# New slots for the second block's steps beside the attention heads, and score maxima turned as 16 rows of 128

## The chip, the cores and the metric

The kernel runs on one core of one Trainium2 chip. The metric is the time of one launch on the device in microseconds (us), as a median over runs.

## What is computed

Eight independent samples (B = 8), each 512 rows of 512 numbers, go through two transformer blocks, one after the other. Cut to what matters here:

```python
# block 0 (16 heads of 32; every linear layer quantises its input rows to 8 bits and its weight to -1, 0, 1)
xn = rmsnorm(x, g1) * (1 + scale) + shift
q, k, v = heads(bitlinear(xn, w_qkv, b_qkv))
attn = softmax(q @ k.T * 32 ** -0.5)              # 16 heads, each 512 x 512
x = x + bitlinear(attn @ v, w_proj, b_proj)
x = x + bitlinear(gelu(bitlinear(adaln(x), w_fc1)), w_fc2)
# block 1 (one head of 512, plain weights)
h = film(rmsnorm(x), cond)
x = x + softmax(Q(h) @ K(h).T * 512 ** -0.5) @ V(h) @ proj_w + proj_b
x = x + gelu(film(rmsnorm(x), cond) @ mlp_w1 + mlp_b1) @ mlp_w2 + mlp_b2
```

## The kernel before

The instruction streams of all engines are written out by hand. `both(i, j)` on every engine issues block 0 of sample i together with block 1 of sample j = i - 1. So there are nine rounds: sample 0 alone with the preparation of the weights, seven rounds of both, and block 1 of the last sample alone. A round of both lasts some 248 us.

**Precision.** Numbers go to TensorE (PE) as two bf16 parts, high and low. ScalarE (ACT) writes the high part, and VectorE (DVE) or GpSimd (POOL) the low part, as the difference. A product in block 1 is three matmuls for each of four chunks (`three_terms`, L1430 to L1432), twelve of 128x512.

**The heads' loop.** Its order is that of `slots()`: slots (c, n), with n from 0 to 23 for c = 0 and from 0 to 15 for c = 1 to 4. In a slot the PE issues, in this order: block 1's steps that `PE_AT` names for the slot, a late q or k product of block 0 (`LATE_QK`), the scores by query (`scores_by_query`, L1193), the scores by key (`scores_by_key`, L1243, for c > 0), a head's weighing of the values (`weigh_values`, L1278, 32 matmuls), and the turn of a group's maxima (`turn_maxima`, L1212). A group is four heads, so 16 score tiles. The scores by query only serve to find each row's maximum; `maxima` reads them on DVE, two tiles at once for the first 24 (L1202, banks 0 to 3), one at a time for the rest (L1205, banks 0 and 1). The scores by key have two rows more in the contraction, the negated maximum as high and low part, which lie in partitions STACK and STACK + 1 of `q_stack`. ACT takes their exponential (L1250), and the low part of each of the 64 tiles is formed by DVE or POOL (L1261; the lists `LOW_DVE` and `LOW_POOL`). A head's values are weighed seven slots (six in the first group) after the slot of its first exponential, by `VALUES_AT`.

**The way of the maxima of a group c:** DVE writes them into `neg_max` [128 rows, 4 row tiles, 4 heads]. PE turns them, one matmul of 4 columns for each row tile, into a bank of 4 rows (heads) of 512. ACT copies the high part (`max_high`, L1219), DVE takes the low part (`max_low`, L1226), and SyncE (SP) sends each of the two by a DMA of its own into one partition of `q_stack` (`stack_maxima`, L1232 and L1234). The PE waits for both at slot (c + 1, 0) (`scores_by_key`, n == 0). The slots are in `MAX_AT`, `HIGH_AT` and `LOW_AT`.

**Block 1 in the same loop.** Scores of row tiles 2 and 3 (`s1`, `S_AT`), the turned probabilities (`turn_p1`, L1600, `PT_AT`), the four attention outputs (`proj1`, `PROJ_AT`), squares and norms on ACT (L1442, L1458), the turn into columns with film (`turn_y1`, L1477, `TURN_AT`), and eight quarters of the first two products of the first MLP layer (`M_AT`). Their readers on DVE and ACT have slots of their own (`PT_READ`, `PROJ_READ`), or slots derived from the PE's. Engines are independent queues: a slot of DVE is not at the time of the same slot of PE, but its instructions wait in this order.

SP's queue in the loop: spill and stack of q and k parts of group 2 (L1144, L1146, L1155), `stack_maxima` 0, spill 3, `stack_maxima` 1, stack 3, `stack_maxima` 2 and 3.

```python
EXTRA_DVE = (17, 22, 25, 30, 34, 38)
EXTRA_POOL = (48, 52, 56, 60)
LOW_DVE = [e for e in range(KC * HEADS) if (e >= FIRST_DVE or e in EXTRA_DVE) and e not in EXTRA_POOL]   # FIRST_DVE = 42
```

Of the kernel before, what the change touches and what calls it, by code (L numbers as in the profile page):

```python
# [231 lines left out]
def two_blocks(nc, a, out):  # L232
# [6 lines left out]
    with ExitStack() as ctx:  # L239
# [2105 lines left out]
```

## Time and profile before

| | us |
|---|---|
| median of 3 runs | 2208.48 |
| lowest, highest | 2206.46, 2213.61 |
| the profiled execution | 2211.1 |
| its span | 2209.3 |
| PE busy | 1975.2 (89%) |
| DVE busy | 1537.1 (70%) |
| ACT busy | 1088.2 (49%) |
| POOL busy | 807.1 (37%) |

The span runs from the first to the last instruction; 1.8 us lie around it. A matmul's duration in the rows includes its drain: matmuls of 512 columns start 0.22 us apart and are listed with 0.38 us. So idle time of the PE is read from the gaps in the brackets of its rows and from starts, not from the sum of durations.

### The profile page before, as it was taken

How to read it: one execution, taken by the hardware profiler on the slowest of the kernel's cores; microseconds unless marked ns; L12 is line 12 of the kernel's file. 1: busy time of each engine (PE TensorE's matmuls, PEld its weight loads, DVE VectorE, ACT ScalarE, POOL GpSimd, SP SyncE). 2: the span in 40 equal slices, each digit the busy share in tenths (PEclk: the TensorE clock that was granted, in tenths of full speed). 3: DMA queues.
4: the chain of work that ended last, by engine and by line, in shares of the span. 5: the costliest groups of instructions: out<-in, count | busy, mean ns of one | idle time of the engine just before them, and what ended most of it. 6: DMA issues, size and time to landing. Idle time of an engine off the chain costs nothing.

```text
span 2209.3 us, 34388 instructions
## 1 busy us (share of the span) xinstructions
PE 1975.2 (89%) x12991; PEld 981.8 (44%) x12991; DVE 1537.1 (70%) x2667; ACT 1088.2 (49%) x1962; POOL 807.1 (37%) x705
## 2 busy tenths in 40 slices
PE   4787868899988998899988998899988998899989
PEld 3354334544444444544444444544444444544434
DVE  5666567885788767875788767875788767875422
ACT  4475543753456443753456343753456343753230
POOL 2173433741246213741245213741246213741021
PEclk8899889999999999999999999999999999999999
DMA  8442552023321333023321333023321332013212
GB/s 307 146 164 105 191 195 100 26 87 96 129 73 40 105 115 101 26 88 96 132 68 40 107 113 101 26 87 96 131 71 40 109 111 101 26 62 97 91 38 96
DMA packets 152027, 216.97 MB, mean 98 GB/s; under 512 B 74172, under 2 KB 115424, under 8 KB 139704
## 3 DMA queue, kind: packets, MB, share of 16 engines
q1 hardware_dynamic: 144088, 191.66, 26.3%
q10 hardware_dynamic: 7776, 23.10, 2.8%
q8 instruction: 106, 1.74, 0.3%
q14 instruction: 57, 0.47, 0.1%
HBM read 161.97 MB, written 35.72 MB: 89 GB/s over the span
## 4 chain that ended last, share of the span: by engine, by line
PE 55%; DVE 25%; ACT 9%; issue 6%; POOL 3%; DMA 1%; SPq 0%; ACTq 0%; DVEq 0%; POOLq 0%
PE banks L1430 10%; PE banks L1432 10%; PE banks L1431 10%; PE banks L1388 5%; PE banks L1331 4%; DVE memory L1205 4%; PE banks L1278 4%; DVE memory L1202 3%; PE banks L1243 2%; DVE memory L1016 2%; ACT memory L1250 2%; PE banks L1102 2%; PE banks L1193 2%; PE banks L1313 1%; DVE memory L1031 1%
## 5 line engine op out<-in xcount | busy, mean ns | idle before, releaser
L1430 PE MATMUL banks<-memory 128*128 128x512 bf16 x1536 | 586.1, 382 | 25.9 <-DVE memory L1678 5.9
L1431 PE MATMUL banks<-memory 128*128 128x512 bf16 x1536 | 585.5, 381 | 0.0
L1432 PE MATMUL banks<-memory 128*128 128x512 bf16 x1536 | 585.1, 381 | 0.0
L1261 POOL TENSOR_TENSOR memory<-memory 128x512 bf16<-128x512 f32 x332 | 375.4, 1151 | 371.0 <-ACT memory L1250 370.0
L1250 ACT ACTIVATE memory<-banks 128x512 f32<-128x512 f32 x512 | 290.4, 598 | 131.3 <-PE banks L1243 129.1
L1656 POOL TENSOR_TENSOR memory<-memory 128x512 bf16<-128x512 f32 x128 | 153.8, 1204 | 459.1 <-DVE memory L1651 459.1
L1193 PE MATMUL banks<-memory 96*128 96x512 bf16 x512 | 188.6, 395 | 72.8 <-DVE memory L1205 41.4
L1430 PEld LDWEIGHTS banks<-memory 128*128 128x128 bf16 x1536 | 150.7, 98 | 215.3 <-issue 40.0
L1205 DVE TENSOR_REDUCE memory<-banks 128x1 f32<-128x512 f32 x320 | 207.6, 679 | 42.4 <-PE banks L1193 41.9
L1432 PEld LDWEIGHTS banks<-memory 128*128 128x128 bf16 x1536 | 150.8, 98 | 184.0 <-issue 4.4
L1431 PEld LDWEIGHTS banks<-memory 128*128 128x128 bf16 x1536 | 150.9, 98 | 170.5 <-issue 3.5
L1243 PE MATMUL banks<-memory 98*128 98x512 bf16 x512 | 187.6, 391 | 13.3 <-ACT memory L1250 6.7
L1645 ACT ACTIVATE memory<-banks,memory 128x512 f32<-128x512 f32 x128 | 87.5, 684 | 205.1 <-PE banks L1432 135.2
L1678 DVE TENSOR_TENSOR memory<-banks,memory 128x512 f32<-128x512 f32 x128 | 88.2, 689 | 121.3 <-PE banks L1432 120.8
L1278 PEld LDWEIGHTS banks<-memory 128*128 128x128 bf16 x4096 | 145.7, 100 | 47.0 <-issue 24.2
L1261 DVE TENSOR_TENSOR memory<-memory 128x512 bf16<-128x512 f32 x180 | 141.4, 818 | 35.8 <-ACT memory L1250 35.1
L1278 PE MATMUL banks<-memory 128*128 128x66 bf16 x4096 | 152.0, 197 | 14.8 <-issue 12.4
L1651 DVE CAST memory<-memory 128x512 bf16<-128x512 f32 x128 | 67.8, 542 | 93.1 <-ACT memory L1645 92.1
L1331 PE MATMUL banks<-memory 128*128 128x512 fp8e4 x512 | 118.8, 386 | 13.6 <-issue 10.2
L1202 DVE TENSOR_REDUCE memory<-banks 128x2 f32<-128x1024 f32 x96 | 116.8, 1217 | 17.9 <-PE banks L1193 17.1
L1388 PE MATMUL banks<-memory 128*128 128x512 fp8e4 x512 | 118.0, 384 | 8.4 <-DMA memory<-memory 8.4
L1470 POOL TENSOR_TENSOR memory<-memory 128x512 f32<-128x512 f32 x64 | 80.5, 1272 | 119.2 <-DVE memory L1078 112.1
(173 smaller groups left out, 2775.4 us busy)
## 6 DMA issues: line engine op xcount, KB each, us to landing
memory<-weight_parts SPq DMA_DIRECT2D x80, 1024.0 KB, 4.8
memory<-head_parts SPq DMA_DIRECT2D x192, 128.0 KB, 2.6
head_parts<-memory SPq DMA_DIRECT2D x64, 256.0 KB, 2.2
memory<-in_x SPq DMA_DIRECT2D x32, 256.0 KB, 3.4
memory<-ada_rows SPq DMA_DIRECT2D x16, 512.0 KB, 4.5
memory<-in_L_cond_w_fc ACTq DMA_DIRECT2D x2, 4096.0 KB, 14.9
memory<-in_L_cond_mlp_w SPq DMA_DIRECT2D x8, 1024.0 KB, 9.2
weight_parts<-memory SPq DMA_DIRECT2D x8, 1024.0 KB, 5.8
```

Of the source, the lines that this page charges most:

```text
L1193: mm = pe.matmul(banks[:, b], q_stack[0:STACK, c % STACKS, j, t * P:(t + 1) * P], k_stack[0:STACK, c % STACKS, j], start=True, stop=True)
L1202: dve.tensor_reduce(neg_max[:, c % 2, t - 1:t + 1, j], banks[:, b - 1:b + 1], AX.X, ALU.max, negate=True).then_inc(free[b].sem, 1)
L1205: dve.tensor_reduce(neg_max[:, c % 2, t, j:j + 1], banks[:, b], AX.X, ALU.max, negate=True).then_inc(free[b].sem, 1)
L1243: pe.matmul(banks[:, b], k_stack[0:rows, c % STACKS, j, kt * P:(kt + 1) * P], q_stack[0:rows, c % STACKS, j], start=True, stop=True).then_ ...
L1250: act.activation(expo[:, e % RING], banks[:, b], ACT.Exp, scale=HEAD_SCALE).then_inc(free[b].sem, 1)
L1261: eng.tensor_tensor(prob_lo[:, e % RING], expo[:, e % RING], prob_hi[:, e % RING], ALU.subtract).then_inc(ok.sem, 1)
L1278: mm = pe.matmul(banks[:, b, at:at + VALUE], part[:, (h * TT + kt) % RING, t * P:(t + 1) * P], values[:, kt, h], start=(kt == 0 and part i ...
L1331: mm = pe.matmul(banks[:, b], xq[:, k, t * P:(t + 1) * P], w0_fc1[:, k, n * D:(n + 1) * D], start=(k == 0), stop=(k == KC - 1))
L1388: mm = pe.matmul(banks[:, b], hid_turned[t % 2][:, f], w0_fc2[:, f], start=(f == 0), stop=(f == FC - 1))
L1430: pe.matmul(bank, lh, rh, start=(k == 0), stop=False)
L1431: pe.matmul(bank, lh, rl, start=False, stop=False)
L1432: mm = pe.matmul(bank, ll, rh, start=False, stop=(k == KC - 1))
```

## The change

Three things change. (1) `neg_max` is laid out [128 rows, 4 heads, 4 row tiles]; one matmul of 16 columns turns a group's maxima into 16 rows of 128, so `max_high` and `max_low` work on 16 x 128 instead of 4 x 512, and each of the two DMAs moves 16 rows of 256 bytes instead of 4 of 1024 into the same 4096 bytes of one partition. (2) The slots of block 1's steps and of the late q and k steps move, and readers get lists of their own (`FILM_*`, `PT_HIGH`, `PT_LOW`, `S_MAX`, `S_EXP`). `s1` and `proj1` can now be issued in quarters; the four quarters of each stand in one slot. (3) The low parts of 20 instead of 24 tiles are formed by DVE, of 44 instead of 40 by POOL; `ACT_CUTS`, `DVE_CUTS` and `BOUNDS` shift a few steps of block 1 after the loop.

```diff
-LATE_QK = {(0, 6): ("q", 2), (0, 12): ("k", 2), (1, 3): ("q", 3), (1, 6): ("k", 3)}
-LATE_SCALE = {(0, 5): ("q", 2), (0, 9): ("k", 2), (1, 3): ("q", 3), (1, 7): ("k", 3)}
-LATE_HIGH = {(0, 5): ('q', 2), (0, 9): ('k', 2), (1, 4): ('q', 3), (1, 9): ('k', 3)}
-LATE_LOW = {(0, 6): ('q', 2), (0, 12): ('k', 2), (1, 5): ('q', 3), (1, 8): ('k', 3)}
+LATE_QK = {(0, 4): ('q', 2), (0, 12): ('k', 2), (1, 2): ('q', 3), (1, 8): ('k', 3)}
+LATE_SCALE = {(0, 4): ('q', 2), (0, 9): ('k', 2), (1, 2): ('q', 3), (1, 7): ('k', 3)}
+LATE_HIGH = {(0, 4): ('q', 2), (0, 9): ('k', 2), (1, 4): ('q', 3), (1, 10): ('k', 3)}
+LATE_LOW = {(0, 5): ('q', 2), (0, 12): ('k', 2), (1, 4): ('q', 3), (1, 10): ('k', 3)}
...
-M_AT = ((3, 8), (3, 11), (3, 14), (4, 1), (4, 4), (4, 7), (4, 10), (4, 13))
+M_AT = ((3, 11), (3, 13), (3, 15), (4, 2), (4, 3), (4, 5), (4, 9), (4, 15))
...
-ACT_CUTS = (1, 6, 8, 9)
-DVE_CUTS = (2, 3, 4, 6, 8, 9, 10, 11, 12)
-BOUNDS = (14, 14, 15, 16, 17, 18, 19, 20, 21, 22, 23, 24, 25, 26, 27, 27)
+ACT_CUTS = (1, 6, 7, 10)
+DVE_CUTS = (2, 3, 3, 6, 7, 9, 10, 11, 12)
+BOUNDS = (14, 14, 15, 17, 17, 18, 19, 20, 20, 21, 23, 23, 24, 26, 27, 27)
...
-TURN_AT = ((2, 7), (2, 9), (2, 11), (2, 13))
-NORM_AT = ((1, 14), (1, 15), (2, 0), (2, 1))
-SQUARE_AT = ((1, 4), (1, 6), (1, 8), (1, 10))
-PT_AT, PT_READ = (((0, 3), (0, 10), (0, 15)), ((0, 2), (0, 11), (0, 14)))
-S_AT = ((0, 4), (0, 7))
-PROJ_AT, PROJ_READ = (((0, 16), (0, 21), (1, 0), (1, 5)), ((0, 15), (0, 22), (0, 23), (1, 5)))
+TURN_AT, FILM_FULL, FILM_HIGH, FILM_LOW = (((2, 5), (2, 7), (2, 9), (2, 12)), ((2, 5), (2, 7), (2, 9), (2, 12)), ((2, 6), (2, 8), (2, 10), (2, 13)), ((2, 7), (2, 9), (2, 11), (2, 14)))
+NORM_AT = ((1, 14), (1, 15), (2, 0), (2, 2))
+SQUARE_AT = ((1, 0), (1, 1), (1, 5), (1, 11))
+PT_AT, PT_HIGH, PT_LOW = (((0, 3), (0, 10), (0, 16)), ((0, 2), (0, 11), (0, 15)), ((0, 2), (0, 11), (0, 15)))
+S_AT, S_MAX, S_EXP = (((0, 4), (0, 4), (0, 4), (0, 4), (0, 8), (0, 8), (0, 8), (0, 8)), ((0, 4), (0, 8)), ((0, 4), (0, 8)))
+PROJ_AT, PROJ_READ = (((0, 16), (0, 16), (0, 16), (0, 16), (0, 20), (0, 20), (0, 20), (0, 20), (1, 0), (1, 0), (1, 0), (1, 0), (1, 5), (1, 5), (1, 5), (1, 5)), ((0, 17), (0, 20), (0, 23), (1, 5)))
...
-MAX_AT = {(0, 17): 0, (1, 8): 1, (2, 11): 2, (3, 10): 3}
-HIGH_AT = {(0, 17): 0, (1, 9): 1, (2, 10): 2, (3, 9): 3}
-LOW_AT = {(0, 17): 0, (1, 11): 1, (2, 11): 2, (3, 12): 3}
+MAX_AT = {(0, 18): 0, (1, 9): 1, (2, 9): 2, (3, 9): 3}
+HIGH_AT = {(0, 18): 0, (1, 11): 1, (2, 10): 2, (3, 9): 3}
+LOW_AT = {(0, 18): 0, (1, 13): 1, (2, 11): 2, (3, 10): 3}
...
-EXTRA_DVE = (17, 22, 25, 30, 34, 38)
-EXTRA_POOL = (48, 52, 56, 60)
+EXTRA_DVE = (12, 14, 17, 23, 34, 38, 39)
+EXTRA_POOL = (46, 48, 49, 50, 54, 56, 57, 60, 62)
...
-        neg_max = fp32(2, TT, G)
+        neg_max = fp32(2, G, TT)
...
-            for t in range(TT):
-                mm = pe.transpose(banks[0:G, b, t * P:(t + 1) * P], neg_max[:, c % 2, t], ident)
-            mm.then_inc(full[b].sem, 1)
+            pe.transpose(banks[0:HEADS, b, 0:P], neg_max[:, c % 2].rearrange("p j t -> p (j t)"), ident
+                         ).then_inc(full[b].sem, 1)
...
-            act.activation(max_hi[0:G], banks[0:G, b], ACT.Copy).then_inc(max_parts.sem, 1)
+            act.activation(max_hi[0:HEADS, 0:P], banks[0:HEADS, b, 0:P], ACT.Copy).then_inc(max_parts.sem, 1)
...
-            dve.tensor_tensor(max_lo[0:G], banks[0:G, b], max_hi[0:G],
+            dve.tensor_tensor(max_lo[0:HEADS, 0:P], banks[0:HEADS, b, 0:P], max_hi[0:HEADS, 0:P],
...
-            sp.dma_start(q_stack[STACK:STACK + 1, c % STACKS], max_hi[0:G]).then_inc(max_in[c].sem, 16)
+            sp.dma_start(q_stack[STACK:STACK + 1, c % STACKS].rearrange("p j (t n) -> p (j t) n", t=TT),
+                         max_hi[0:HEADS, 0:P]).then_inc(max_in[c].sem, 16)
```

The DMA of `max_lo` changes in the same way.

## Rows read from the trace of the kernel before

**Rows 1.** The page: busy time of each engine.
```profile
PE 1975.2 (89%) x12991; PEld 981.8 (44%) x12991; DVE 1537.1 (70%) x2667; ACT 1088.2 (49%) x1962; POOL 807.1 (37%) x705
```

**Rows 2.** Waits of the PE from 600 to 1900 us: total, times, longest.
```profile
PE banks L1193 <- DVE memory L1205: 32.4, 67, 1.2
PE banks L1193 <- DVE memory L1202: 22.3, 24, 1.1
```

**Rows 3.** Round of sample 3: window, length, busy PE PEld DVE ACT POOL, clock, DMA, GB/s.
```profile
852.30:877.42 25.12, 21.15 (x100) 9.65 (x101) 21.99 (x30) 4.80 (x10) 0.00 (x0) 1.00 0.43 138
877.42:896.31 18.89, 15.96 (x153) 7.92 (x152) 15.20 (x30) 12.95 (x28) 14.53 (x15) 1.00 0.09 30
896.31:914.59 18.28, 14.99 (x182) 8.72 (x181) 17.20 (x32) 16.91 (x34) 15.73 (x15) 1.00 0.15 45
914.59:923.75 9.16, 7.61 (x87) 4.23 (x84) 8.01 (x17) 5.30 (x11) 7.31 (x7) 0.81 0.01 2
923.75:944.25 20.50, 18.40 (x282) 11.57 (x279) 15.83 (x34) 16.96 (x34) 8.24 (x8) 1.00 0.01 3
944.25:1086.00 141.75, 138.60 (x687) 64.68 (x684) 96.74 (x164) 60.59 (x102) 40.84 (x37) 1.00 0.31 101
```

**Rows 4.** The fourth of these stages, in the round of sample 2.
```profile
667.60:676.80 9.20, 7.34 (x90) 3.60 (x86) 8.77 (x19) 5.81 (x13) 8.89 (x8) 1.00 0.01 2
```

**Rows 5.** The turns of the maxima in three rounds: durations, first and last start.
```profile
L1212 PE MATMUL banks<-memory x16: 269/272/274, 622.2 to 677.8; 128*4 128x128 f32 x16
L1212 PE MATMUL banks<-memory x16: 269/272/274, 869.2 to 926.0; 128*4 128x128 f32 x16
L1212 PE MATMUL banks<-memory x16: 269/272/274, 1117.5 to 1174.4; 128*4 128x128 f32 x16
```

**Rows 6.** Timeline, slots (0, 5) to (1, 0): start, duration, what; the gap before it.
```profile
858.88 0.75 DVE L1126 SCALAR_TENSOR_TENSOR memory<-memory 128x512 bf16<-128x512 f32 x1 [0.79 <-ACT memory L1138]
869.20 0.60 PE L1212 MATMUL banks<-memory 128*4 128x128 f32 x4 [0.20 <-DVE memory L1202]
871.38 0.38 PE L1193 MATMUL banks<-memory 96*128 96x512 bf16 x1 [1.14 <-DVE memory L1202]
874.60 1.23 DVE L1202 TENSOR_REDUCE memory<-banks 128x2 f32<-128x1024 f32 x1 [1.65 <-PE banks L1193]
878.05 0.38 PE L1243 MATMUL banks<-memory 98*128 98x512 bf16 x1 [0.25 <-DVE memory L1202]
```

**Rows 7.** Small reads of a bank, one line each: shortest, median and longest in ns.
```profile
L1219 ACT ACTIVATE memory<-banks x32: 569/586/586, 95.7 to 1919.7; 4x512 bf16<-4x512 f32 x32
L1291 ACT ACTIVATE memory<-banks x128: 249/277/398, 118.2 to 1937.8; 128x128 f32<-128x128 f32 x128
L1226 DVE TENSOR_TENSOR memory<-banks,memory x32: 668/672/679, 96.3 to 1921.4; 4x512 bf16<-4x512 f32 x32
L1298 DVE TENSOR_TENSOR memory<-banks,memory x128: 247/253/261, 121.2 to 1938.3; 128x128 f32<-128x128 f32 x128
```

**Rows 8.** The low parts of the exponentials on POOL and DVE: shortest, median, longest.
```profile
L1261 POOL TENSOR_TENSOR memory<-memory x332: 1030/1039/2097, 106.1 to 1933.5; 128x512 bf16<-128x512 f32 x166
L1261 DVE TENSOR_TENSOR memory<-memory x180: 669/679/1464, 172.1 to 1935.9; 128x512 bf16<-128x512 f32 x180
```

**Rows 9.** Timeline around slot (2, 0): the maxima of group 1 leave, and their first reader.
```profile
893.57 0.58 SPq L1234 DMA_DIRECT2D memory<-memory  x1
896.53 0.38 PE L1243 MATMUL banks<-memory 98*128 98x512 bf16 x1
896.46 0.72 ACT L1458 ACTIVATE memory<-memory 128x512 f32<-128x512 f32 x1 [0.75 <-POOL memory L1449]
```

**Rows 10.** Timeline around slot (4, 0) and at the loop's end.
```profile
928.73 0.57 SPq L1234 DMA_DIRECT2D memory<-memory  x1
930.84 0.38 PE L1243 MATMUL banks<-memory 98*128 98x512 bf16 x1
943.29 1.12 PE L1278 MATMUL banks<-memory 128*128 128x66 bf16 x32 [1.53 <-issue]
```

More of the change, by code:

```diff
@@ L1201, in maxima @@
             if paired(c, n):
-                dve.tensor_reduce(neg_max[:, c % 2, t - 1:t + 1, j], banks[:, b - 1:b + 1], AX.X, ALU.max,
+                dve.tensor_reduce(neg_max[:, c % 2, j, t - 1:t + 1], banks[:, b - 1:b + 1], AX.X, ALU.max,
                                   negate=True).then_inc(free[b].sem, 1)
             else:
-                dve.tensor_reduce(neg_max[:, c % 2, t, j:j + 1], banks[:, b], AX.X, ALU.max,
+                dve.tensor_reduce(neg_max[:, c % 2, j, t:t + 1], banks[:, b], AX.X, ALU.max,
                                   negate=True).then_inc(free[b].sem, 1)
@@ L1560, in qv_low, with s1 @@
                                   ALU.subtract).then_inc(free[b].sem, 1)
-        def s1(pe, i, t):
+        def s1(pe, i, t, ks=range(KC)):
             if t == 0:
                 all_done(pe, plan1, [("q", c) for c in range(KC)], i, ("s", t))
-            b = take(pe, plan1, ("s", t), i)
+            b = take(pe, plan1, ("s", t), i) if ks[0] == 0 else plan1["s", t][0]
             cols = slice(t * P, (t + 1) * P)
             three_terms(pe, banks[:, b], lambda k: (act_q[:, 0, k, cols], act_q[:, 1, k, cols]),
-                        lambda k: (act_h[:, 0, k], act_h[:, 1, k]), full[b])
+                        lambda k: (act_h[:, 0, k], act_h[:, 1, k]), full[b], ks)
         def max1(dve, i, t):
@@ L1613, in p_low, with proj1 @@
                               act_k[:, 0, :, t * P:(t + 1) * P], ALU.subtract).then_inc(free[b].sem, 1)
-        def proj1(pe, i, t):
-            all_done(pe, plan1, [("v", TT - 1), ("pT", t)], i, ("proj", t))
-            b = take(pe, plan1, ("proj", t), i)
+        def proj1(pe, i, t, ks=range(KC)):
+            if ks[0] == 0:
+                all_done(pe, plan1, [("v", TT - 1), ("pT", t)], i, ("proj", t))
+            b = take(pe, plan1, ("proj", t), i) if ks[0] == 0 else plan1["proj", t][0]
             cols = slice(t * P, (t + 1) * P)
             three_terms(pe, banks[:, b], lambda k: (act_k[:, 0, k, cols], act_k[:, 1, k, cols]),
-                        lambda k: (act_v[:, 0, k], act_v[:, 1, k]), full[b])
+                        lambda k: (act_v[:, 0, k], act_v[:, 1, k]), full[b], ks)
         def proj_add1(dve, i, t):
@@ L1698, in two_blocks @@
             (at, ("pT", t + 1)) for t, at in enumerate(p_at)]
-        PE_AT = place(*s_p(S_AT, PT_AT), *((at, ("proj", t)) for t, at in enumerate(PROJ_AT)),
+        quarters = lambda name, first, places: [(at, (name, first + k // KC, (k % KC,))) for k, at in enumerate(places)]
+        PE_AT = place(*quarters("s", 2, S_AT), *((at, ("pT", t + 1)) for t, at in enumerate(PT_AT)),
+                      *quarters("proj", 0, PROJ_AT),
                       *((at, ("turn", k)) for k, at in enumerate(TURN_AT)), *((at, (*M[k // KC], (k % KC,))) for k, at in enumerate(M_AT)))
-        DVE_AT = place(*s_p(S_AT, PT_READ), *((at, ("proj", t)) for t, at in enumerate(PROJ_READ)),
-                       *((later(at, 2), ("low", k)) for k, at in enumerate(TURN_AT)))
-        ACT_AT = place(*s_p(S_AT, PT_READ), *((at, ("square", t)) for t, at in enumerate(SQUARE_AT)),
+        DVE_AT = place(*s_p(S_MAX, PT_LOW), *((at, ("proj", t)) for t, at in enumerate(PROJ_READ)),
+                       *((at, ("low", k)) for k, at in enumerate(FILM_LOW)))
+        ACT_AT = place(*s_p(S_EXP, PT_HIGH), *((at, ("square", t)) for t, at in enumerate(SQUARE_AT)),
                        *((at, ("norm", t)) for t, at in enumerate(NORM_AT)),
-                       *((at, ("full", k)) for k, at in enumerate(TURN_AT)),
-                       *((later(at, 1), ("film", k)) for k, at in enumerate(TURN_AT)))
+                       *((at, ("full", k)) for k, at in enumerate(FILM_FULL)),
+                       *((at, ("film", k)) for k, at in enumerate(FILM_HIGH)))
         @block.sync
```

3 lines of the change are left out of this document (2 added, 1 removed).

## The prediction

> **What bounds the kernel now.** I read the page first: the PE is busy for 89% of the span, DVE for 70% [rows 1]. That says that the PE is near its limit as a mean, and not where. So next the busy times by stage. The reader is to see two kinds of stage in a round of 248 us. In the long one, the MLPs and projections, the PE is busy for 138.6 of 141.75 us and nothing but less PE work would help. In the five stages of the heads' loop (92 us) it is not: DVE is busy for 22.0 of 25.1 us in the first and for 17.2 of 18.3 in the third, where ACT has 16.9 as well, and the fourth runs at a granted clock of 0.81 [rows 3]. The waits of the PE agree: the two largest are the score tiles that wait until DVE has read the maxima of earlier ones, 32.4 and 22.3 us in 5.3 rounds, so some 10 us in a round [rows 2]. Last I read the timeline of the loop for the links of that chain [rows 6, 9, 10].
>
> **First stage, slots (0, 4) to (1, 0).** DVE stands still for 25.12 - 21.99 = 3.1 us [rows 3], and two waits make 2.44 of it [rows 6].
> - 0.79 us before the low part of q: DVE scales q in slot (0, 5), ACT must make the high part (L1138), and DVE's next instruction is the low part. The new order has q's product and scaling in slot (0, 4) and the low part in (0, 5), with the maxima of a pair (1.2 us by the row of L1202) between them, longer than the wait. It goes. Next late there is p's high part, which waits behind ACT's work; I keep 0.3 us for it.
> - 1.65 us before the pair 20, 21: the PE issued score 20 first, had to wait 1.14 us for its bank, then ran the second attention output (12 matmuls at 0.22 us, 2.6 us) and then score 21. DVE had nothing to read. The new order issues that output at (0, 20), ahead of score 20, at a time when the PE would wait for a bank anyway. Both waits lie over each other and the 1.65 goes.
> - `max_low` falls from 0.67 us for 4 x 512 to about 0.25, if a read of 16 x 128 costs what one of 128 x 128 does; the nearest row of the old width is 0.67, of the new 0.253 [rows 7]. I take 0.25, since in these rows the length and not the partitions sets the time (4 x 512 costs 672 ns). Gain 0.4 on DVE, with 0 as other end.
>
> Sum 0.79 + 1.65 + 0.4 - 0.3 = 2.5 us a round. Ends: 1.0 if only one wait goes, 3.5 if all idle goes. What was hidden, the way of group 0's maxima, must now be over earlier: `max_low` moves one slot back, to (0, 18), but DVE is ahead by then, and some 4 us remain to slot (1, 0).
>
> **Second stage, c = 1.** DVE takes tiles 12 and 14 (2 x 0.68 us [rows 8]) and saves 0.4: 1.0 us more work in a stage where it is idle for 3.7 [rows 3]. POOL loses tile 12 (1.04 us) that stands ahead of the norm's square root, for which ACT waits 0.75 us [rows 9]; that wait goes. But `max_low` of group 1 moves from (1, 11) to (1, 13). Two slots are 2 x 18.89 / 16 = 2.4 us. Between the issue of this DMA and its reader at (2, 0) there were 3.0 us [rows 9]; 3.0 - 2.4 + 0.4 = 1.0 is left. How long the landing takes the trace doesn't say; at slot (4, 0) it was over within 930.84 - 928.73 = 2.1 us of the issue's start [rows 10]. So the PE may wait up to 1.1 us. The matmuls behind it wait too, but DVE still has a score tile to read. SP waits as well, with the stacking of group 3 behind it, which was tied to the last key score of group 0 at (1, 15) anyway. I set 0 for this stage, from -1.1 to +0.7.
>
> Here a rule of the Trainium skill speaks against the change. The 4096 bytes of each DMA go in 16 pieces of 256 bytes instead of 4 of 1024. "DMA: Bandwidth & Descriptors", section "Specifications", says that below 512 bytes a transfer doesn't reach line rate and is read, modified and written. By it the landing would be longer than the old 2.1 us; by the rows, where 4 KB are nothing beside the fixed part, it would be the same. No row shows which.
>
> **Third stage, c = 2.** DVE's tiles go from four (17, 22, 25, 30) to two (17, 23): 1.36 us less, 0.4 less for `max_low`, of 17.2 busy in 18.3. ACT with 16.9 is the next bound, so at most 1.4 can be had, and the turned rows (`TURN_AT` at (2, 5), with the last norm in (2, 2)) may make the PE wait for ACT. I take 0.8, from 0 to 1.4.
>
> **Fourth stage, clock.** Sample 3's round ran this stage at 0.81 of full speed, sample 2's at 1.00 [rows 3, 4]: part of it at 1.2 instead of 2.4 GHz, after the PE had waited for DVE again and again. The round without the fall lasted 869.2 - 622.2 = 247.0 us, the next, with it, 1117.5 - 869.2 = 248.3 [rows 5]. So a fall costs 1.3 us. With fewer waits ahead of it I expect it to be rarer: 0.6 a round, from -0.7 to 1.3.
>
> **Fifth stage, (3, 8) to the end of the loop.** The PE is nearly full, ACT 17.0 of 20.5. The turn of the maxima is in its path: four matmuls in 0.60 us of which the first takes 0.27, so 0.11 each [rows 5, 6]; three of them are 0.3 us. The eight quarters of the MLP's first layer are the same work in other slots. At the end the PE stands still for 1.53 us before the last head [rows 10], until DVE has formed three low parts in a row. Now POOL forms tile 62 beside DVE's 61 and 63, and the last quarter at (4, 15) sits where the PE would wait. I take 0.6, from 0 to 1.5.
>
> **The rest.** The small copy on ACT (0.586 to 0.277 us [rows 7]) is off the path. `ACT_CUTS`, `DVE_CUTS`, `BOUNDS` shift readers after the loop by one step; the 138.6 us of PE work cover them [rows 3]. Without that cover a reader one step late costs the PE one product, about 1 us; I take 0.
>
> **Sum.** 2.5 + 0 + 0.8 + 0.6 + 0.3 + 0.6 = 4.8 us a round, 33.6 in seven. The first round, whose DVE is busy with the weights, gives some 1 us by its four turns; the last has no heads. 2211.1 - 34.6 = 2176.5 for an execution like the profiled one. It was 2.6 us above the median, so I say 2175 beside 2208.48 (-1.5%). The lower ends of the terms give 1.0 - 1.1 + 0 - 0.7 + 0 + 0 = -0.8, so no gain; the upper ends 3.5 + 0.7 + 1.4 + 1.3 + 0.3 + 1.5 = 8.7, so 2147. All ends at once are unlikely.
>
> **Rivals.**
> 1. *The gain moves on.* The first stage gains only half and DVE or ACT takes back the rest in c = 1 and 2: about 2 us a round, 2194. For it: ACT is at 16.9 of 18.3 in c = 2. Against: the two waits in the first stage have no other owner. 0.20.
> 2. *The small rows land late.* If 16 pieces take twice the 2.1 us, the PE waits 4.2 - 1.0 = 3.2 us at (2, 0) instead of 1.1, so 2.1 x 7 = 15 us come back: 2190. This is the page's rule above. 0.05.
> 3. *POOL becomes the bound: slower.* It forms 44 tiles instead of 40. Its median is 1.04 us, but single ones took 2.10, while DVE's went from 0.68 to 1.46 [rows 8]. POOL's tiles must fit in the last four stages, 66.8 us. At 1.04 they are 46, at 1.7 they are 75, with 1.2 for the root 76: 9 us a round over, less the first stage's 2.5, so about 2255. It decides from about 1.6 us a tile on. Against: POOL's busy time in these stages is 45.8 us for 45 instructions [rows 3]. With lesser mishaps of that sort (a reader that now comes first in its queue and waits) 0.09. The skill's "GPSIMD Engine Reference", section "Specifications", has POOL and DVE share their way to memory when DVE has two inputs there; the longest durations of both agree, and fewer such DVE instructions would ease it.
> 4. *Nothing that can be measured.* The loop is held by something that the lists don't touch: within 6.6 us. 0.07.
>
> My forecast has the rest, 0.59. A difference below 0.3%, 6.6 us, can't be told from none. Faster 0.59 + 0.20 + 0.05 = 0.84, same 0.07, slower 0.09. The range is 2154 to 2206: its top takes in rivals 1 and 2 and leaves out most of 3 and 4; below it lie only most of the upper ends at once.
>
> **What would show it.** Turn: one matmul of 128 x 16, about 0.27 us; `max_low` and `max_high` near 0.25. First stage: no wait of DVE before L1126 and none of over 0.5 before the pair 20, 21; the time from group 0's turn to the first key score falls from 878.05 - 869.20 = 8.9 us by two or more, though the turn itself comes a slot later. Slot (2, 0): a wait of L1243 for a DMA of up to 1 us; over 2 would be rival 2. Clock 1.00 in the fourth stage of more rounds. Last head: a gap under 1 us. The forecast is wrong if a round isn't shorter than 246 us, and rival 3 holds if L1278 waits for POOL.

## The result: 1.5% faster, as forecast, but only partly by the forecast terms

| | before | after |
|---|---|---|
| median, us | 2208.59 | 2175.09 |
| lowest, highest | 2206.46, 2213.61 | 2173.14, 2179.12 |
| the profiled execution, its span | 2211.1, 2209.3 | 2179.12, 2177.3 |
| ratio, with its 95% interval | | 0.9847 [0.9826, 0.9869] |

The forecast was 2175. The page of the kernel after, beside [rows 1]:

```profile
span 2177.3 us, 34196 instructions
PE 1959.1 (90%) x12895; PEld 974.4 (45%) x12895; DVE 1531.2 (70%) x2639; ACT 1076.0 (49%) x1962; POOL 847.4 (39%) x733
```

The span is 32.0 us shorter. Where: the first product of block 1 in a round (128x2, L1531 before, L1532 after) starts at 343.62 us in sample 1's round and at 2074.14 in the last before, at 345.25 and 2042.76 after. So the first round is 1.6 us longer, seven rounds are 33.0 us shorter (4.72 each, where the prediction had 4.8), and the tail is 0.6 shorter.

For what follows a round is cut at six starts: that first product; the first key score; key scores 16, 32 and 48, with which c = 2, 3 and 4 begin; the last head's weighing; the next round's first product. These are lengths between starts, so drains don't matter. The first stage is longer than that of [rows 3], since it begins before the loop. Means over all seven rounds of the one profiled execution of each kernel:

| stage | before | after | gained | the prediction's terms |
|---|---|---|---|---|
| 1: to the first key score | 38.87 | 36.24 | 2.63 | 2.5 |
| 2: c = 1 | 19.14 | 17.46 | 1.68 | 0 |
| 3: c = 2 | 17.85 | 17.88 | -0.03 | 0.8 |
| 4: c = 3 | 15.50 | 13.63 | 1.87 | 0.6, turn 0.3 |
| 5: c = 4, to the last head | 12.55 | 13.16 | -0.61 | last head 0.6 |
| 6: to the next round | 143.31 | 144.12 | -0.81 | 0 |

The sum is 4.73, the 4.72 above but for rounding. Stage 6 of the last round has no next sample and is 137.5 us before and 137.4 after; in the other six it is 144.29 as a mean before and 145.24 after. "A fall" is below a stretch within a stage in which the granted clock is 0.50, that is 1.2 instead of 2.4 GHz; it shows as a mean clock under 1 in the stage.

The windows of one clean round after (length; busy PE, PEld, DVE, ACT, POOL; clock; DMA; GB/s), to be held against [rows 3]:

```profile
588.38:624.11 35.73, 32.25 (x183) 15.34 (x182) 31.86 (x50) 11.85 (x22) 4.64 (x5) 1.00 0.46 148
624.11:641.34 17.23, 15.73 (x151) 7.75 (x150) 16.34 (x30) 12.63 (x29) 15.25 (x15) 1.00 0.10 33
641.34:658.67 17.33, 13.92 (x177) 8.60 (x178) 16.95 (x32) 16.30 (x35) 15.93 (x15) 1.00 0.17 47
658.67:672.41 13.74, 11.96 (x162) 6.58 (x161) 12.86 (x27) 10.21 (x21) 10.15 (x10) 1.00 0.01 2
672.41:685.57 13.16, 11.05 (x165) 6.72 (x162) 10.38 (x19) 11.06 (x23) 10.72 (x9) 1.00 0.01 3
685.57:830.37 144.80, 141.22 (x720) 66.18 (x721) 96.70 (x167) 61.80 (x104) 42.30 (x38) 1.00 0.31 100
```

The granted clock is 1.00 in the fourth window. It was so in all seven rounds after; before it was 0.89 in five of the seven. DVE is busy for all but 0.4 to 0.9 us of the second to fourth windows, so it is mostly what these stages wait for. In c = 1 that is new: there it stood idle for 3.7 us before [rows 3]. The waits of the PE from 580 to 1870 us, 5.3 rounds, against [rows 2]:

```profile
PE banks L1193 <- DVE memory L1205: 29.0, 58, 1.5
PE banks L1193 <- DVE memory L1202: 11.8, 12, 1.1
PE banks L1279 <- POOL memory L1262: 8.8, 5, 1.8
...
PE banks L1389 <- DMA memory<-memory: 3.2, 4, 1.5
PE banks L1244 <- DMA memory<-memory: 3.0, 4, 1.5
```

and, not among [rows 2], the wait for the last head before:

```profile
PE banks L1278 <- issue: 7.7, 5, 1.5
```

The waits for the pairs' maxima (L1202) are halved. The wait of the last head is 8.8 us where it was 7.7; that the row names POOL is misleading (experiment 6). Two waits are new, both for a DMA.

**The first stage.** DVE's timeline after, with PE's below it, against [rows 6]:

```profile
849.05 0.74 DVE L1126 SCALAR_TENSOR_TENSOR memory<-memory 128x512 bf16<-128x512 f32 x1
...
861.31 0.27 DVE L1225 TENSOR_TENSOR memory<-banks,memory 16x128 bf16<-16x128 f32 x1
861.51 1.20 DVE L1202 TENSOR_REDUCE memory<-banks 128x2 f32<-128x1024 f32 x1
...
863.58 2.34 DVE L1202 TENSOR_REDUCE memory<-banks 128x2 f32<-128x1024 f32 x2
```

```profile
859.21 0.27 PE L1211 MATMUL banks<-memory 128*16 128x128 f32 x1
...
866.09 0.38 PE L1244 MATMUL banks<-memory 98*128 98x512 bf16 x1
```

There is no wait before L1126 (0.79 before), and the last pairs are read back to back where DVE had waited 1.65 us. The turn is one matmul of 0.27 us, the low part takes 0.27 us, and from the turn to the first key score it is 866.09 - 859.21 = 6.9 us, where it was 8.9.

### The profile page after: what moved, and what is told of

Its sections match the earlier page's. It is cut to its first block, busy times and chain, and to the rows that moved or that the text cites. A ratio compares the mean times of both kernels' runs of the same rounds, so it can differ in the third digit from the quotient of the medians.

```text
span 2177.3 us, 34196 instructions
## 1 busy us (share of the span) xinstructions
PE 1959.1 (90%) x12895; PEld 974.4 (45%) x12895; DVE 1531.2 (70%) x2639; ACT 1076.0 (49%) x1962; POOL 847.4 (39%) x733
## 3 DMA queue, kind: packets, MB, share of 16 engines
q8 instruction: 105, 1.72, 0.3%
HBM read 161.97 MB, written 35.72 MB: 91 GB/s over the span
## 4 chain that ended last, share of the span: by engine, by line
PE 56%; DVE 24%; ACT 9%; issue 5%; POOL 4%; DMA 2%; ACTq 0%; SPq 0%; DVEq 0%; POOLq 0%
PE banks L1431 10%; PE banks L1433 10%; PE banks L1432 10%; PE banks L1332 5%; PE banks L1389 4%; DVE memory L1205 4%; PE banks L1279 3%; POOL memory L1262 2%; DVE memory L1202 2%; PE banks L1244 2%; PE banks L1193 2%; DVE memory L1016 2%; PE banks L1102 2%; ACT memory L1251 2%; DVE memory L1031 2%
## 5 line engine op out<-in xcount | busy, mean ns | idle before, releaser
L1262 POOL TENSOR_TENSOR memory<-memory 128x512 bf16<-128x512 f32 x360 | 412.3, 1168 | 302.2 <-ACT memory L1251 298.8
L1658 POOL TENSOR_TENSOR memory<-memory 128x512 bf16<-128x512 f32 x128 | 153.0, 1197 | 481.0 <-DVE memory L1653 481.0
L1193 PE MATMUL banks<-memory 96*128 96x512 bf16 x512 | 184.0, 392 | 57.9 <-DVE memory L1205 37.8
L1205 DVE TENSOR_REDUCE memory<-banks 128x1 f32<-128x512 f32 x320 | 207.2, 679 | 22.3 <-PE banks L1193 21.9
L1653 DVE CAST memory<-memory 128x512 bf16<-128x512 f32 x128 | 60.9, 485 | 111.1 <-ACT memory L1647 110.1
L1202 DVE TENSOR_REDUCE memory<-banks 128x2 f32<-128x1024 f32 x96 | 115.3, 1214 | 10.1 <-PE banks L1193 9.3
```

What stands on the lines that cost most here:

```text
L1193: mm = pe.matmul(banks[:, b], q_stack[0:STACK, c % STACKS, j, t * P:(t + 1) * P], k_stack[0:STACK, c % STACKS, j], start=True, stop=True)
L1202: dve.tensor_reduce(neg_max[:, c % 2, j, t - 1:t + 1], banks[:, b - 1:b + 1], AX.X, ALU.max, negate=True).then_inc(free[b].sem, 1)
L1205: dve.tensor_reduce(neg_max[:, c % 2, j, t:t + 1], banks[:, b], AX.X, ALU.max, negate=True).then_inc(free[b].sem, 1)
L1262: eng.tensor_tensor(prob_lo[:, e % RING], expo[:, e % RING], prob_hi[:, e % RING], ALU.subtract).then_inc(ok.sem, 1)
```

## The experiments

Each was run beside the kernel before on the same chip, which gave medians of 2208.08 to 2210.43 us; the ratios are to that. All are built from one of the two kernels of the case. Lengths and counts of rounds come from one profiled execution of each. "Stage" means the stages of the table above.

### 1. The turn alone

Before, with the new layout of `neg_max`, the one matmul of 16 columns, its parts and its DMAs; slots and lists are the old ones.

> The kernel before with the turn of the maxima alone changed (one matmul of 16 columns, 16 x 128), all slots and lists old. Theory A, the parts add up by engine time: 0.4 us of DVE in each of the first three stages and 0.3 us of PE in the last, 1.5 us a round, so 10 to 12 us faster than before, about 2197. Theory B, the narrow maxima carry the whole change because their way to the key scores is what ends the stages: 25 us faster or more, about 2183. Theory C, their way is hidden and DVE has slack: within 3 us of before. A and B differ in the wait at slot (2, 0): there is none in any case, with the old slots.

Measured: 2219.7 us (2214.32 to 2222.86), ratio 1.0032 [1.0018, 1.0047]. The turn alone makes the kernel slower, and none of the three theories holds. c = 1 is 1.1 us shorter (18.08; 0.4 shorter beside rounds without a fall), but c = 2 is 0.9 longer (18.79) and c = 3 1.6 longer (17.09), and in c = 3 the clock is 0.90 in all seven rounds. The timeline of this stage in one of them:

```profile
922.19 1.04 POOL L1262 TENSOR_TENSOR memory<-memory 128x512 bf16<-128x512 f32 x1 [1.28 <-ACT memory L1251]
...
922.58 1.19 DVE L1503 TENSOR_TENSOR memory<-memory 128x512 bf16<-128x512 f32 x1
...
923.45 2.67 POOL L1262 TENSOR_TENSOR memory<-memory 128x512 bf16<-128x512 f32 x2 [0.22 <-ACT memory L1251]
923.70 1.52 DVE L1262 TENSOR_TENSOR memory<-memory 128x512 bf16<-128x512 f32 x1
...
925.88 0.60 PE L1193 MATMUL banks<-memory 96*128 96x512 bf16 x1 [2.56 <-DVE memory L1205]
```

The same two DVE instructions in before, and the POOL tile that starts beside them:

```profile
914.85 0.67 DVE L1502 TENSOR_TENSOR memory<-memory 128x512 bf16<-128x512 f32 x1
915.44 0.67 DVE L1261 TENSOR_TENSOR memory<-memory 128x512 bf16<-128x512 f32 x1
L1261 POOL TENSOR_TENSOR memory<-memory x1: 2092/2092/2092, 914.9 to 914.9; 128x512 bf16<-128x512 f32 x1
```

The reader is to see the chain: DVE's two instructions with two inputs in memory take 1.19 and 1.52 us instead of 0.67 twice, the PE waits 2.56 us for its bank, and then its matmuls last 0.60 instead of 0.38 us: the clock is at 1.2 GHz instead of 2.4. In before it was POOL that paid at this place: its tile at 914.93 took 2.09 us, the next two 1.03 each.

Which of the two pays can mostly be read from the starts: the one that starts second. In before DVE's 914.85 is ahead of POOL's 914.93; here POOL's 922.19 is ahead of DVE's 922.58. The whole trace of after says the same. Its 91 DVE instructions of this form (two inputs in memory, 128x512) that start while no POOL instruction of this form runs take 0.67 to 0.69 us. The 102 that start with over 0.15 us of a POOL instruction left take this rest and 0.55 us more, within 0.01 us, 0.76 to 1.57 in all. Before's trace has an exception at two places of every round: DVE keeps its 0.67 us and POOL takes 1.7 to 2.1, where DVE starts 0.13 us after POOL, or where POOL already waits for the DVE instruction ahead (915.44 above).

### 2. Everything but the turn

After, with the old turn of four matmuls of 4 columns.

> The changed kernel with the old turn (four matmuls of 4 columns, 4 x 512), all new slots. Theory A: 8 to 12 us slower than the changed kernel, about 2184. Theory B: nearly back to before, over 2200. It also tells whether the small rows land late: the changed kernel waits up to 1.5 us for a DMA at slot (2, 0). If 16 pieces of 256 bytes are what lands late, this kernel waits less there although its low part is ready 0.4 us later; if the landing has a fixed time, it waits 0.4 us more.

Measured: 2174.45 us (2168.84 to 2176.2), ratio 0.9835 [0.982, 0.985]; after's interval, [0.9826, 0.9869], overlaps it. Neither theory holds. So the whole gain is in slots, lists and cuts. Beside after, the first stage without a fall of the clock is 0.4 us longer (36.13, after 35.72), c = 2 and c = 3 are shorter (17.23 and 13.38, after 17.88 and 13.63): what the turn saves it gives back later. In a round without a fall stages 1 to 5 are 97.20 us together here and 97.19 after.

Key score (2, 0) starts 1.74 to 1.81 us after the issue of the second small DMA in all seven rounds here, with 4 pieces of 1024 bytes and waits of 0.1 to 0.2 us. With 16 pieces of 256 bytes it is 1.66 to 1.83 in five rounds of seven, with the same small waits, and 3.08 and 2.76 in the other two.

### 3. The new slots of the first stage alone

Before, with these slots and nothing else:

```diff
-LATE_QK = {(0, 6): ("q", 2) ...     +LATE_QK = {(0, 4): ("q", 2) ...      (scale, high, low likewise)
-PT_AT, PT_READ = ((0, 3), (0, 10), (0, 15)), ((0, 2), (0, 11), (0, 14))
+PT_AT, PT_READ = ((0, 3), (0, 10), (0, 16)), ((0, 2), (0, 11), (0, 15))
-S_AT = ((0, 4), (0, 7))
+S_AT = ((0, 4), (0, 8))
-PROJ_AT, PROJ_READ = ((0, 16), (0, 21), (1, 0), (1, 5)), ((0, 15), (0, 22), (0, 23), (1, 5))
+PROJ_AT, PROJ_READ = ((0, 16), (0, 20), (1, 0), (1, 5)), ((0, 17), (0, 20), (0, 23), (1, 5))
 MAX_AT, HIGH_AT, LOW_AT: (0, 17) -> (0, 18)
```

> The kernel before with only the new slots of the first stage: q's late product, scaling, high and low part, the second block's scores, turned probabilities and attention outputs, and group 0's maxima. Theory A: DVE's waits of 0.79 and 1.65 us go, 2.1 to 2.5 us a round, 15 to 17 us faster than before, about 2192. Rival, the gain moves on: the stage is shorter by as much, but the stages after it take half or more back; then at most 8 us faster, 2200 or more.

Measured: 2203.67 us (2197.79 to 2206.82, 10 runs), ratio 0.9967 [0.9957, 0.9978]. The stage gains what was forecast, 38.74 to 36.13 us in rounds without a fall, and the rival holds for the rest. In three of seven rounds the clock falls in this stage (37.8), and in c = 2 it is at 0.81 to 0.92 in five of seven, which makes that stage 2.3 us longer as a mean (20.10). A gain of 2.6 us where it is made is one of 1.1 in the round: (2071.78 - 349.01) / 7 = 246.1 from the starts of the rounds, before 247.2. The first round is 5.4 us longer than before's.

### 4. Its two halves

Only q's slots:

> The kernel before with only the late q product, its scaling and its parts moved to the new slots (0, 4), (0, 4), (0, 4), (0, 5) (scores and attention outputs stay). Only the lengths of the first stage and the waits of DVE are read, not the time of the launch. Theory A (the two waits of the first stage are two causes): DVE's wait of 0.79 us before L1126 is gone, the wait of 1.65 us before the pair 20, 21 stays, and the first stage without a fall of the clock is 0.5 to 0.9 us shorter than before's 38.74. Rival B (the wait before L1126 is slack that the later one takes up): the later wait grows by as much and the stage stays within 0.3 us of 38.7.

and only the others of the first stage:

> The kernel before with the new slots of the first stage other than those of the late q (scores of row tile 3, turned probabilities, second attention output ahead of score 20, the turn of group 0 at (0, 18)). Only lengths and waits of the first stage are read. Theory A (two causes): the wait of 1.65 us before the pair 20, 21 is gone, that of 0.79 us before L1126 stays, and the first stage without a fall of the clock is 1.5 to 2.2 us shorter than before's 38.74. Rival B (they hang together): it is shorter by all of the 2.6 us that both together gave, or by less than 1 us.

Measured, in one execution of each (2208.85 and 2202.12 us): q's slots alone 38.62 us, the others alone 37.02 (rounds without a fall), both 36.13. So 0.12 and 1.72 add up to 1.84, and both together give 2.61. The first half fits neither theory: the wait before L1126 is gone, but one of 0.68 us for the PE stands one instruction later, the wait of 1.65 us is as it was, and the stage gains 0.12.

```profile
858.14 0.74 DVE L1126 SCALAR_TENSOR_TENSOR memory<-memory 128x512 bf16<-128x512 f32 x1
859.55 1.23 DVE L1202 TENSOR_REDUCE memory<-banks 128x2 f32<-128x1024 f32 x1 [0.68 <-PE banks L1193]
...
874.62 1.23 DVE L1202 TENSOR_REDUCE memory<-banks 128x2 f32<-128x1024 f32 x1 [1.65 <-PE banks L1193]
```

The second half did what its theory A said. In a round without a fall the wait before L1126 is as it was, and DVE waits before none of the last pairs:

```profile
1105.32 0.75 DVE L1126 SCALAR_TENSOR_TENSOR memory<-memory 128x512 bf16<-128x512 f32 x1 [0.79 <-ACT memory L1138]
...
1120.26 2.35 DVE L1202 TENSOR_REDUCE memory<-banks 128x2 f32<-128x1024 f32 x2
```

In the two of its seven rounds in which the clock falls in this stage, 1.5 us of waiting stand before an earlier pair, and the stage is 1.6 us longer. So the 1.65 is a term of its own. The 0.79 isn't: the wait that follows it is one for the PE, and q's slots are worth 0.12 us alone and 0.89 beside the others. The prediction added the two as if they were separate; the sum was right only because both edits were made.

### 5. The old cuts after the loop

After, with the old `ACT_CUTS`, `DVE_CUTS` and `BOUNDS`.

> The changed kernel with the old ACT_CUTS, DVE_CUTS and BOUNDS. In the changed kernel the stretch from the last head to the next round's first product is 145.2 us as a mean and 144.3 before, with waits of up to 1.5 us of the second MLP product for the transposing DMA. Theory A, the new cuts let a load of weights collide with the transpose: these waits go, 0.5 to 0.9 us a round, 3 to 7 us faster than the changed kernel, about 2170. Rival, the waits come from the heads' loop ending at another phase and the cuts are needed for it: no gain or a loss, 2175 or more.

Measured: 2171.61 us (2169.67 to 2173.31), ratio 0.9826 [0.9812, 0.9841]. Its interval overlaps after's, so the gain of 3.5 us that theory A forecast isn't clear of noise, but the traces differ plainly: in the six rounds with a next sample stage 6 is 144.3 us here, and 144.3 to 146.5 after. After, at SP's queue and at the layer's second half:

```profile
1021.69 0.32 SPq L1419 DMA_DIRECT2D memory<-weight_parts  x1
...
1022.95 3.92 SPq L1381 DMA_TRANSPOSE memory<-memory  x1
1030.53 3.61 PE L1389 MATMUL banks<-memory 128*128 128x512 fp8e4 x16 [1.10 <-DMA memory<-memory]
```

and with the old cuts:

```profile
1022.34 1.63 SPq L1381 DMA_TRANSPOSE memory<-memory  x1
1028.65 3.62 PE L1389 MATMUL banks<-memory 128*128 128x512 fp8e4 x16
...
1034.89 0.33 SPq L1419 DMA_DIRECT2D memory<-weight_parts  x1
```

The new cuts put the load of the next weights ahead of the transposing DMA, whose issue then takes 3.92 instead of 1.63 us, and the PE waits for it. The long issue, 3.9 to 4.6 us, comes in all seven rounds after, and 3.7 to 4.4 in all seven of experiment 2, which has the new cuts too; here it is 1.6 in all. The wait of the PE doesn't come in every round: it is there in four of seven after (3.2 us in sum), and experiment 2's stage 6 is 144.26 in all but one. Of the 5.7 us that stage 6 loses after in six rounds, these waits are 3.2; the rest stands mostly in three rounds whose clock falls behind the last head.

### 6. Tile 62 back on DVE

After, with tile 62 taken out of `EXTRA_POOL`.

> The changed kernel with tile 62, of the last head, back on DVE (EXTRA_POOL without 62). In the changed kernel POOL works five tiles in a row of 1.4 us each at the end of the heads' loop, and the PE stands still for 1.8 us ahead of the last head until POOL is done (1.5 us before, waiting for DVE). Theory A, POOL's last tile sets the end: the wait falls to 1.0 to 1.5 us, with the clock falls that follow it in two rounds of seven, 2 to 7 us faster than the changed kernel, about 2171. Rival, both engines share their way to memory and DVE's third tile is stretched by as much: the wait stays within 0.2 us of 1.8, 2175.

Measured: 2175.43 us (2173.65 to 2179.78), ratio 0.9852 [0.9838, 0.9866], no difference to after. The loop's end after, and then DVE's last three tiles before, against the 1.53 us of [rows 10]:

```profile
922.35 6.93 POOL L1262 TENSOR_TENSOR memory<-memory 128x512 bf16<-128x512 f32 x5 [1.00 <-ACT memory L1251]
...
927.03 1.12 PE L1279 MATMUL banks<-memory 128*128 128x66 bf16 x32 [0.34 <-issue]
927.12 2.70 DVE L1262 TENSOR_TENSOR memory<-memory 128x512 bf16<-128x512 f32 x2
...
929.92 1.92 PE L1279 MATMUL banks<-memory 128*128 128x66 bf16 x32 [1.77 <-POOL memory L1262]
...
931.65 0.62 PE L1431 MATMUL banks<-memory 128*128 128x512 bf16 x1
```

```profile
940.89 2.30 DVE L1261 TENSOR_TENSOR memory<-memory 128x512 bf16<-128x512 f32 x3
```

The row names POOL as what ended the wait of 1.77 us, but POOL's last tile is done at 922.35 + 6.93 = 929.28. DVE's is done at 927.12 + 2.70 = 929.82, and the PE starts 0.10 us later. It is so in all seven rounds, and before too the PE starts 0.10 us after DVE (940.89 + 2.30 = 943.19, and 943.29). So the PE still waits for DVE: beside POOL its tiles 61 and 63 take 1.25 and 1.52 us, more than its three took before. With tile 62 on DVE the wait is 1.53 us in all rounds, 0.24 less than after and just above theory A's range, and the time is the rival's.

Stage 5 is 12.92 us instead of 13.16, and with the old lists (next) 12.42. Most of what is left is the wait of 0.34 us one head earlier, also for a tile of DVE's, 59, which takes 1.53 us beside POOL.

### 7. The old lists of tiles

After, with the old `EXTRA_DVE` and `EXTRA_POOL`.

> The changed kernel with the old lists of low parts (24 tiles on DVE, 40 on POOL). My sum had 0.8 us a round from DVE's relief in c = 2 and 0.6 at the loop's end, against 0 in c = 1. Theory A: 5 to 10 us slower than the changed kernel, 2180 to 2185. Rival, POOL is now the engine that is full (15.1 to 16.1 us busy of 17.1 to 17.5 in c = 1 and 2) and the new lists gain nothing: within 3 us, or faster.

Measured: 2181.22 us (2177.72 to 2183.28), ratio 0.9874 [0.986, 0.9887]; 6 us above after, as theory A said. Stage 5 is 0.7 us shorter, but c = 2 is 19.40 us (after 17.88), with the clock at 0.93 to 0.96 in six of seven rounds. The clock is only a part of it: in the one round without a fall c = 2 is 19.04 us, where after has 17.3 to 17.5. So the new lists, which leave DVE two tiles fewer there, are worth 1.5 us or more in c = 2, and the falls come on top.

### 8. Is it really the meeting of DVE and POOL?

Experiment 1, with tile 30 formed by POOL:

```diff
-EXTRA_DVE = (17, 22, 25, 30, 34, 38)
+EXTRA_DVE = (17, 22, 25, 34, 38)
```

> The kernel before with the new turn of the maxima, and tile 30 of the low parts formed by POOL instead of DVE. With the new turn alone (tile 30 on DVE) the kernel took 1.0032 of before; in its c = 3 stage DVE's read of a bank (L1503) and tile 30 ran side by side with POOL and took 1.19 and 1.52 us, the PE then waited 2.56 us for L1205 at slot (3, 2), and the clock was at half in a stretch of this stage in every round. Theory A (this meeting of DVE's and POOL's two-input instructions is what makes the turn alone slower): DVE has 1.5 us less there, the wait of over 2 us is gone, the clock falls in at most half the rounds, the c = 3 stage goes from 17.1 to 15.5 us or less, and the time is 2200 to 2209 us, not above before. Rival B (tile 30 only happens to be there; POOL is as full and the clock falls anyway): c = 3 stays at 16.5 to 17.5 us with the clock falling in nearly every round, and the time stays at 2215 to 2222.

Measured: 2210.02 us (2205.09 to 2213.58, 10 runs), ratio 1.0004 [0.9992, 1.0016]. The loss of 0.3% is gone. c = 3 goes from 17.09 to 14.71 us, and the clock falls there in three of seven rounds instead of all. The two places in this kernel:

```profile
915.33 1.32 DVE L1503 TENSOR_TENSOR memory<-memory 128x512 bf16<-128x512 f32 x1
...
917.32 0.39 PE L1193 MATMUL banks<-memory 96*128 96x512 bf16 x1 [1.24 <-DVE memory L1205]
```

One of the two long instructions is left, and the wait is 1.24 instead of 2.56 us. That is theory A in the stage, and the time is 1 us above its range. It doesn't become a gain, since the first stage now has falls in four rounds of seven and is 0.6 us longer (39.50). The edit also takes a tile of work off DVE, so it doesn't show how much of the effect is the meeting and how much a DVE with less to do.

### 9. Versions that should beat both

(a) After with the old cuts, tile 62 on DVE, and the parts of group 1's maxima at (1, 10) and (1, 11) instead of (1, 11) and (1, 13):

> The changed kernel with three repairs: old cuts after the loop, tile 62 on DVE, and group 1's maxima copied at (1, 10) and (1, 11) instead of (1, 11) and (1, 13). If the repairs add up: 3.5 us from the cuts, 2 to 7 from the last tile, and 1 to 3 from slot (2, 0), where the PE waited 1.1 to 1.5 us for the DMA in two rounds of seven; 2163 to 2169. Rival, what is gained ahead only moves a fall of the clock: 2171 or more.

(b) After with the old turn, the old cuts and tile 62 on DVE:

> New slots, old turn (four matmuls, 4 x 512), old cuts, tile 62 on DVE. The turn alone made the kernel before 7 us slower and its absence cost the changed kernel nothing (2174.45 beside 2175.09). If the turn is worth nothing in any surroundings, this is at or below the combined kernel with the new turn, 2163 to 2169. If its shorter reads on DVE count once the clock stays up, the combined kernel is 2 to 5 us faster than this one.

(c) Version (b) with group 1's parts as in (a):

> All that the runs so far favour: the new slots with the old turn of four matmuls, the old cuts, tile 62 on DVE, and the parts of group 1's maxima at (1, 10) and (1, 11). Theory A (each wait taken away counts by itself): no wait for a DMA at slot (2, 0) or before L1388, a round is 0.1 to 0.3 us shorter than in the same kernel with group 1 at (1, 11) and (1, 13), 2166 to 2171 us. Rival B (what the loop wins is taken back by falls of the clock in the first stage, 1.65 us each, that come and go with any shift): 2170 to 2174, no better than the three kernels at 2170.5 to 2172.

| | us (range) | ratio | stages 1 to 5 | stage 6 |
|---|---|---|---|---|
| a | 2171.96 (2170.36 to 2172.37) | 0.9832 [0.9819, 0.9846] | 36.66, 16.90, 17.88, 13.78, 12.92 | 144.31 |
| b | 2170.46 (2168.32 to 2176.39) | 0.9836 [0.982, 0.9853] | 37.07, 17.61, 16.96, 13.38, 12.92 | 144.30 |
| c | 2182.56 (2181.27 to 2183.33) | 0.988 [0.986, 0.99] | 37.08, 17.30, 18.22, 13.37, 12.92 | 144.6 |

Stage 6 is the mean of the six rounds with a next sample. (a) and (b) are 3 to 5 us under after's median, within overlapping intervals; (a) is where its rival said, not at the 2163 to 2169 of repairs that add up, and (b) beside it shows no worth of the turn. (c) was to be the best of all and is 12 us above (b), a miss for both of its theories. The wait at (2, 0) is gone and c = 1 0.3 us shorter, but c = 2 is 1.3 us longer, 1.05 of it in every round. It isn't the earlier parts by themselves: (a) has them with the new turn, and c = 1 and c = 2 are 34.57 us together in a round without a fall, as in (b), where (c) has 35.37. Only old turn and earlier parts together lose this, and why was not found. The starts of the seven rounds put 8.0 us on the rounds and 1.1 on the first. The other 4.6 us are in the tail after the last loop, which has the same work in both kernels. Its windows, first (b), then (c):

```profile
2036.27:2166.50 130.23, 112.43 (x545) 52.36 (x543) 33.76 (x63) 30.20 (x51) 24.61 (x22) 0.96 0.18 65
```

```profile
2045.41:2180.20 134.79, 116.72 (x534) 53.77 (x543) 33.16 (x63) 30.18 (x51) 24.58 (x22) 0.92 0.17 63
```

The clock was granted 0.92 instead of 0.96 there. Why the same chain of work gets the one or the other wasn't settled; the tails of the other kernels are 130 to 135 us as well.

## Why the prediction was right, and where it wasn't

**First stage, 2.5: right in size, in part wrong in form.** Measured 2.63 as a mean and 3.0 without falls of the clock: 2.6 by the slots (experiment 3) and the 0.4 of the shorter `max_low`. Both waits are gone, as said. "Both waits lie over each other" holds of the PE's and DVE's in one slot. But 0.79 isn't a gain of its own beside the 1.65 (experiment 4). Clock falls of 1.6 us, of which before has one of 0.9 in seven rounds (39.64), came in two.

**c = 1, 0, and c = 2, 0.8: together too low.** Measured 1.68 and -0.03. The start of key score (2, 0), where one ends and the other begins, moves with every wait and fall, so they are better read as one. Without a fall the two take 36.75 us before and 34.56 after: 2.2 for the forecast 0.8. Before has three falls in c = 1 (19.9 to 20.1 instead of 18.5 us), which cost the two stages only 0.5 each. After has two in c = 2, which cost 2.7 each, so 1.65 is left in the mean. Where the 2.2 come from: the turn alone gives nothing (36.75 in experiment 1), everything but the turn gives all (34.57 in experiment 2), and with the old lists 36.1 is left (the one round without a fall in experiment 7). So about 1.5 are the lists' and the rest that of slots; which ones wasn't tried.

**The wait at (2, 0): forecast up to 1.1.** It is there in two forms. Five rounds wait 0.04 to 0.2 us; two wait 1.46 and 1.14. The issues and the reader, first of a usual round and then of the longest wait:

```profile
639.51 0.51 SPq L1234 DMA_DIRECT2D memory<-memory  x1
...
641.34 0.39 PE L1244 MATMUL banks<-memory 98*128 98x512 bf16 x1 [0.20 <-DMA memory<-memory]
...
881.50 0.51 SPq L1234 DMA_DIRECT2D memory<-memory  x1
...
884.58 0.39 PE L1244 MATMUL banks<-memory 98*128 98x512 bf16 x1 [1.46 <-DMA memory<-memory]
```

The trace of after, unlike before's, tells the landing itself: 1.61 to 1.78 us after the issue in the five rounds, 3.03 and 2.71 in these two. The same two rounds wait in experiments 5 to 7. What else is under way in them was not found, so this stays open. In (a) above, with the parts two slots earlier, no round waits.

**Rival 2, that 16 pieces land late: wrong for most rounds, open for two.** The reader starts as soon after the issue with 16 pieces of 256 bytes (1.66 to 1.83 us) as with 4 of 1024 (1.74 to 1.81). The rule of the Trainium skill, "DMA: Bandwidth & Descriptors", section "Specifications", on transfers below 512 bytes does not show there. But the four kernels that have 16 pieces in these slots (after and experiments 5 to 7) all have two late rounds of seven. The two with 4 pieces have none (experiment 2) and one with a wait of 0.55 us (version (b)). With 4 pieces the low part is also ready later, so no run tells what the pieces have to do with it.

**The fourth stage, 0.6 for the clock and 0.3 for the turn: mis-sized, measured 1.87.** Falls in five of seven rounds became none, worth 0.85 in the mean, and rounds without one are 0.9 us shorter besides (14.65 to 13.74). The price of a fall there, 1.3, is borne out: 14.65 and 15.6 to 16.1. The turn has no part in it: with the old turn the stage is 13.38 (experiment 2).

**The turn, 0.3 on the PE and 0.4 on DVE: not in the total.** The durations are as forecast: PE 273 ns, ACT 249, DVE 270, and the first stage has its 0.4. But the turn alone is slower, and the other parts without it are as fast as with it. In before's slots what happens in c = 3, where DVE and POOL meet, costs more than the turn saves (experiments 1 and 8).

**The last head, 0.6: failed, -0.6.** The step that failed is that tile 62 on POOL takes work off DVE's way at the end. DVE's two tiles beside POOL's take 2.70 us, where its three took 2.30, and the PE waits for DVE 0.24 us longer than before (experiment 6). A wait of 0.34 us for DVE's tile 59 comes one head earlier. The row of this wait looks like the sign of rival 3, L1278 waiting for POOL; the ends of the two engines' tiles show that it isn't.

**The rest, 0: failed, -0.81.** "A reader one step late costs the PE one product" was the wrong thing to fear. What came was the order on SP's queue, for somewhat over half of it, and falls of the clock behind the last head in three rounds (experiment 5).

**The first round and the last step of the sum.** The first round was to give 1 us by its turns and is 1.6 longer. And 2176.5 less the 2.6 us named is 2173.9, not the 2175 that was written.

**Rival 1** (the gain moves on) describes experiment 3 well: a gain of 2.6 became one of 1.1. In the whole change c = 3 has no fall and c = 2 two, where with the old lists it has six. That the total met the forecast so closely is partly luck: c = 1 and 2 together, too low by 0.85, and the fourth stage, too low by 1.0, stand against two losses that were not forecast.

The low parts of the exponentials after, against [rows 8]:

```profile
L1262 POOL TENSOR_TENSOR memory<-memory x360: 1032/1039/2062, 108.1 to 1903.2; 128x512 bf16<-128x512 f32 x180
L1262 DVE TENSOR_TENSOR memory<-memory x152: 669/858/1533, 172.2 to 1903.7; 128x512 bf16<-128x512 f32 x152
```

POOL's median stays at 1.04 us, DVE's rises from 0.68 to 0.86: before, 78 of its 180 tiles have no POOL instruction beside them, after 20 of 152, and none of these 98 takes over 0.69 us. DVE's reads of a bank (L1205), which have no input in memory, stay at 0.68 in all kernels. That agrees with what "GPSIMD Engine Reference" of the Trainium skill, section "Specifications", says: the two engines share their way to memory when DVE has two inputs there.

## What to carry to other kernels

Two waits along one chain between two engines need not be two terms: before adding them, ask what the engine waits for once the first is gone. In a loop where PE, DVE and POOL meet all the time, price an edit also by where it puts DVE's instructions with two inputs in memory against POOL's and by which of the two starts first, and read the granted clock of every stage in every round; a stage that gets faster can lose it in the next one. Where a row says who ended a wait, check it against the ends of all engines that the wait is for. And when steps are moved on an engine, write down the order of the DMA issues that hang on them.

## What wasn't expected of the hardware

- A DVE instruction with two inputs in memory (128x512) took 0.67 to 0.69 us alone and up to 1.60 beside POOL; a low part on POOL took 1.04 and up to 2.39. Mostly the one that starts second pays (experiment 1).
- The PE's clock fell to 1.2 GHz within the loop after single waits of 1.46 us (slot (2, 0)), 1.77 us (last head) and 2.56 us (experiment 1). But the 1.77 us are in all seven rounds, and a fall followed in three; and in the first stage of version (b) the clock fell in four rounds whose waits ahead of it are the same as in the three without a fall (37.79 and 36.14 us). What decides it wasn't found. A fall cost 0.9 to 1.7 us of its stage, and up to 3 in c = 2. Its place repeats from round to round in one kernel and changes with small edits: all rounds of c = 3 in experiment 1, six of seven rounds of c = 2 in experiment 7, three of seven first stages in experiment 3.
- A transposing DMA's issue took 1.6 us on SP's queue, and 3.9 to 4.6 right behind the load of the next weights, in all seven rounds after.
